# Half of the first batch's maxima in the self attention block, keys and the first queries made earlier

## What is computed

```
x = layernorm(x + self_attention(x))            # causal, one head, then w_proj
x = layernorm(x + cross_attention(x, ctx))      # 16 heads of 8 channels
x = layernorm(x + ffn(x))                       # silu(w1 x) * (w2 x), gelu(h1 .), gelu(h2 .), w3
# cross attention of a batch:
q, k, v = x @ wq, ctx @ wk, ctx @ wv
scores  = q k^T + bias(bucket(source position - target position))   # 16 x 56 x 1500
out     = softmax(scores) @ v @ wo
```

## Time and profile before

| | us |
|---|---|
| median of 3 runs | 994.24 (991.3 to 995.9) |
| the profiled execution | 997.42 |
| its span | 995.6 |
| TensorE busy | 922.1 |
| VectorE busy | 729.7 |
| ScalarE busy | 608.6 |
| GpSimd busy | 376.5 |

### The profile page before, as it was taken

How to read it: one execution, slowest core, us unless ns; L and a number is a source line. 1 busy time by engine, 2 the same in 40 slices (tenths; PEclk the granted TensorE clock), 3 DMA queues, 4 the chain that set the end, 5 groups by cost and what they waited for, 6 DMA issues and landing times.

```text
span 995.6 us, 26073 instructions
## 1 busy us (share of the span) xinstructions
PE 922.1 (93%) x10410; PEld 647.2 (65%) x10410; DVE 729.7 (73%) x1705; ACT 608.6 (61%) x1423; POOL 376.5 (38%) x317
## 2 busy tenths in 40 slices
PE   6766699999999999999999999999999998999996
PEld 3544477767677777676776667777777766555564
DVE  5657778888888888888888888888888884710023
ACT  2322377777777777777777777777777767632232
POOL 7300444455555544444555555544444400000000
PEclk9867899999999999999999999999999999999998
DMA  7729766766666676666666666666677503000001
GB/s 206 243 79 176 178 183 181 200 206 182 180 194 186 188 209 193 197 202 197 194 205 176 182 195 181 193 195 206 203 192 204 151 8 121 1 1 0 1 10 28
DMA packets 56324, 154.96 MB, mean 156 GB/s; under 512 B 23234, under 2 KB 35322, under 8 KB 53114
## 3 DMA queue, kind: packets, MB, share of 16 engines
q1 hardware_dynamic: 55820, 152.44, 53.8%
q10 hardware_dynamic: 384, 0.86, 0.3%
HBM read 110.03 MB, written 42.63 MB: 153 GB/s over the span
## 4 chain that ended last, share of the span: by engine, by line
PE 74%; ACT 7%; DVE 3%; issue 2%; DMA 2%; POOL 1%; SPq 1%; ACTq 0%; DVEq 0%; POOLq 0%
PE ps L113 15%; PE ps L877 12%; PE ps L847 12%; PE ps L603 10%; PE ps L930 8%; PE ps L925 7%; PE ps L886 3%; PE ps L597 2%; ACT e_sb L1060 2%; ACT kpart L1033 2%; ACT k_left L1042 1%; ACT vals L1017 1%; DVE cmax L123 1%; PE ps L613 1%; DMA qst<-qslots 1%
## 5 line engine op out<-in xcount | busy, mean ns | idle before, releaser
L1060 ACT ACTIVATE e_sb<-ps 128x448 f32<-128x448 f32 (+1 forms) x768 | 382.7, 554 | 129.5 <-PE ps L847 68.7
L123 DVE TENSOR_REDUCE cmax<-ps 112x1 f32<-112x512 f32 x512 | 330.8, 680 | 56.8 <-PE ps L113 56.5
L113 PE MATMUL ps<-kst,qst 111*112 111x512 bf16 (+1 forms) x768 | 267.8, 390 | 7.1 <-PEq L132 2.8
L847 PEld LDWEIGHTS ps<-qst,kst 114*128 114x128 bf16 (+1 forms) x3072 | 194.8, 101 | 103.8 <-issue 36.0
L847 PE MATMUL ps<-qst,kst 114*128 114x112 bf16 (+1 forms) x3072 | 229.4, 213 | 15.3 <-ACT e_sb L1060 10.9
L120 DVE CUSTOM_DVE_ANT_0 near_out<-ps,near_nat 112x476 bf16<-112x476 f32 x256 | 157.0, 651 | 37.2 <-PE ps L113 34.6
L1105 POOL TENSOR_TENSOR kpart<-k_left,kpart 128x500 bf16<-128x500 f32 x90 | 102.2, 1136 | 205.4 <-ACT k_left L1042 205.4
L877 PE MATMUL ps<-e_sb,vals 128*32 128x168 f32 (+1 forms) x3072 | 149.5, 312 | 0.0
L1111 POOL TENSOR_TENSOR kpart<-k_left,kpart 128x500 bf16<-128x500 f32 x90 | 125.9, 1399 | 7.1
L113 PEld LDWEIGHTS ps<-kst,qst 111*112 111x112 bf16 x768 | 85.5, 131 | 48.2 <-issue 20.7
L930 PEld LDWEIGHTS ps<-wv,ctxt 128*128 128x128 f32 (+1 forms) x768 | 102.1, 193 | 8.1 <-issue 1.2
(11 more groups left out here) (124 smaller groups left out, 918.9 us busy)
## 6 DMA issues: line engine op xcount, KB each, us to landing
kst<-kparts SPq DMA_DIRECT2D x192, 375.0 KB, 6.8
kparts<-kpart SPq DMA_DIRECT2D x90, 375.0 KB, 2.7
ctxt<-in_ctxT SPq DMA_DIRECT2D x31, 750.0 KB, 8.1
qst<-qslots SPq DMA_DIRECT2D x192, 28.0 KB, 7.1
qslots<-qst SPq DMA_DIRECT2D x4, 672.0 KB, 11.5
kparts<-kst SPq DMA_DIRECT2D x6, 375.0 KB, 3.3
qslots<-kst SPq DMA_DIRECT2D x24, 56.0 KB, 4.4
kst<-in_h SPq DMA_DIRECT2D x1, 1024.0 KB, 5.6
```

The costliest lines, as they stand in the source:

```text
L113: return nc.tensor.matmul(dst[0:TT, 0:hi - lo], m.qst[0:M_ROW, r, p, :], m.kst[0:M_ROW, r, p, lo:hi], start=True, stop=True)
L123: return nc.vector.tensor_reduce(m.cmax[:, r, c, p:p + 1], src[0:TT, 0:BOUND[c + 1] - BOUND[c]], AX.X, ALU.max)
L847: mm = nc.tensor.matmul(st_ps[0:K, w % ST_BANKS, p * TT:(p + 1) * TT], m.kst[0:AUG, u % RING, 4 * h + p, j * P:j * P + K], m.qst[0:AUG, u ...
L1060: nc.scalar.activation(e_sb[0:K, j % E_RING, h * HALF:(h + 1) * HALF], st_ps[0:K, w % ST_BANKS, 0:HALF], ACT.Exp).then_inc(s_ex, 1)
```

## The change

- Maxima 0 to 11 of batch 0 are made in the self attention block: 0 to 3 at the start of step 7, 4 to 7 at the start of step 8, 8 to 11 behind step 8, on TensorE and on VectorE, in two PSUM banks (4 and 5). `max_items` leaves them out of the cross attention block.
- The keys of batch 1 are made at the start of step 6 rather than 5; their split, which VectorE did behind stage 2 of the last group (step 5), stands at the start of step 7, ahead of the first maxima.
- Stage 6 stands earlier within its step, on TensorE, ScalarE and VectorE.
- The bias of the self attention's values is added by ScalarE to the product with the values (the weights of a row sum to one) and no longer by VectorE to the values; the copy of the values out of PSUM goes from VectorE to ScalarE.
- On the sync queue the context of batch 1, `wv` and `sel` are loaded right behind near_nat; the queries of batch 0 are stacked right behind the store of group 0's; the store and stacking of batch 1's keys come behind the store of group 1's queries.

```diff
+SA_MAX = 12
-        bqk, bv, bproj, mask = sb("bqk", [C, 2]), sb("bv", [T, C]), sb("bproj", [TT, C]), sb("mask", [T, T])
+        bqk, bv, bproj, mask = sb("bqk", [C, 2]), sb("bv", [C, 1]), sb("bproj", [TT, C]), sb("mask", [T, T])
-        K_AT, K_BANK = {1: 0, 5: 1}, (6, 2)
+        K_AT, K_BANK = {1: 0, 6: 1}, (6, 2)
+        MAX_AT, MAX_BANK = {7: (0, 4), 8: (4, 8), NG + 5: (8, SA_MAX)}, (4, 5)
# sync queue
-            sp.dma_start(bv[:, :], d["b_v"].broadcast_to([T, C])).then_inc(s_in, 16)
+            sp.dma_start(bv[:, :], d["b_v"].rearrange("o c -> c o")).then_inc(s_in, 16)
...
+            sp.dma_start(m.ctxt[:, 1, :], d["ctxT"][C:2 * C, :]).then_inc(m.s_ctx[1], 16)
+            sp.dma_start(m.wv[:, :], d["wv"]).then_inc(m.s_w, 16)
+            for i in range(2):
+                sp.dma_start(m.sel[:, i, :], d["sel"][i]).then_inc(m.s_w, 16)
...
-            sp.dma_start(m.ctxt[:, 1, :], d["ctxT"][C:2 * C, :]).then_inc(m.s_ctx[1], 16)
-            sp.dma_start(m.wv[:, :], d["wv"]).then_inc(m.s_w, 16)
-            for i in range(2):
-                sp.dma_start(m.sel[:, i, :], d["sel"][i]).then_inc(m.s_w, 16)
-            store_k(1)
             sp.wait_ge(s_q3, 1)
             sp.wait_ge(s_qz[0], 16)
             store_q(sp, m, 0)
+            sp.wait_ge(m.s_qd[0], 16 * 6)
+            stack_q(sp, d, m, 0, 0, m.s_ql[0])
+            sp.wait_ge(s_q3, 2)
+            sp.wait_ge(s_qz[1], 16)
+            store_q(sp, m, 1)
+            store_k(1)
             sp.wait_ge(s_kw, 96)
             sp.wait_ge(s_mem, 3)
             stack_k(sp, d, m, 1, m.s_kl[1])
-            sp.wait_ge(m.s_qd[0], 16 * 6)
-            for n in range(SA_K):
-                stack_q(sp, d, m, n, n, m.s_ql[n])
-            sp.wait_ge(s_q3, 2)
-            sp.wait_ge(s_qz[1], 16)
-            store_q(sp, m, 1)
+            stack_q(sp, d, m, 1, 1, m.s_ql[1])
# TensorE
+            def maxima(first, end):
+                if first == 0:
+                    pe.wait_ge(m.s_ql[0], Q_LOAD)
+                    pe.wait_ge(m.s_kl[0], 96)
+                    pe.wait_ge(s_pte, NG)
+                for n in range(first, end):
+                    if n >= 2:
+                        pe.wait_ge(m.s_mr, n - 1)
+                    max_scores(nc, m, ps[:, MAX_BANK[n % 2], :], 0, n // PAIRS, n % PAIRS).then_inc(m.s_mx, 1)
-            for g, st in schedule((5, 1, 3, 4, 0, 2, 6)):
+            for g, st in schedule((5, 1, 3, 6, 4, 0, 2)):
...
+                if st == "start" and g in MAX_AT:
+                    maxima(*MAX_AT[g])
+            maxima(*MAX_AT[NG + 5])
# ScalarE
-            for g, st in schedule((5, 3, 1, "pt", 4, 0, 6)):
+            for g, st in schedule((5, 3, 6, 1, "pt", 4, 0)):
...
+                    act.wait_ge(s_v, g + 1)
+                    nc.scalar.copy(v[:, g, :, :], ps[0:T, 2:4, :].rearrange("p a (b c) -> p (a b) c", b=4)).then_inc(s_ve, 1)
-                    nc.scalar.copy(at[:, g, :], ps[:, 6, 0:GT]).then_inc(s_oe, 1)
+                    nc.scalar.activation(at[:, g, :], ps[:, 6, 0:GT], ACT.Identity, bias=bv[:, 0:1]).then_inc(s_oe, 1)
# VectorE
+            def maxima(first, end):
+                if first == 0:
+                    dve.wait_ge(s_un, 32)
+                for n in range(first, end):
+                    dve.wait_ge(m.s_mx, n + 1)
+                    reduce_scores(nc, m, ps[:, MAX_BANK[n % 2], :], 0, n // PAIRS, n % PAIRS).then_inc(m.s_mr, 1)
-            for g, st in schedule((2, 1, 4, 0, "x1", 6)):
+            for g, st in schedule((2, 1, 6, 4, "x1")):
...
+                if (g, st) == (7, "start"):
+                    dve.wait_ge(s_kf, 6)
+                    nc.vector.tensor_tensor(kpart[:, 1, :], k_left, kpart[:, 0, :], ALU.subtract).then_inc(s_kr, 1)
...
+                if st == "start" and g in MAX_AT:
+                    maxima(*MAX_AT[g])
-                if st == 0:
-                    dve.wait_ge(s_v, g + 1)
...
-                    if g == NG - 1:
-                        dve.wait_ge(s_kf, 6)
-                        nc.vector.tensor_tensor(kpart[:, 1, :], k_left, kpart[:, 0, :], ALU.subtract).then_inc(s_kr, 1)
...
+            maxima(*MAX_AT[NG + 5])
# cross attention block
-                if live(g, u + lag):
+                if live(g, u + lag) and (u + lag > 0 or n >= SA_MAX):
-                if n == 0:
+                if n == 0 or batch(g, u + lag) == 0:
```

More of the change, by code:

```diff
@@ L435, in _ @@
             dve.wait_ge(s_in, NIN)
-            for g, st in schedule((2, 1, 4, 0, "x1", 6)):
+            for g, st in schedule((2, 1, 6, 4, "x1")):
                 if (g, st) == (1, "start"):
                     dve.wait_ge(s_ld, NLD)
+                if (g, st) == (7, "start"):
+                    dve.wait_ge(s_kf, 6)
+                    nc.vector.tensor_tensor(kpart[:, 1, :], k_left, kpart[:, 0, :], ALU.subtract).then_inc(s_kr, 1)
+                    dve.wait_ge(s_kr, 4)
+                    nc.vector.tensor_tensor(k_left, k_left, kpart[:, 0, :], ALU.subtract).then_inc(s_kr, 1)
+                    dve.wait_ge(s_kr, 5)
+                    nc.vector.tensor_tensor(kpart[:, 2, :], k_left, kpart[:, 1, :], ALU.subtract).then_inc(s_kr, 1)
+                if st == "start" and g in MAX_AT:
+                    maxima(*MAX_AT[g])
                 if st == "start":
@@ L442, in _ @@
                 bc = lambda a: a[:, g, :].unsqueeze(2).broadcast_to([T, GB, T])
-                if st == 0:
-                    dve.wait_ge(s_v, g + 1)
-                    nc.vector.tensor_tensor(v[:, g, :, :], ps[0:T, 2:4, :].rearrange("p a (b c) -> p (a b) c", b=4),
-                                            bv[:, :].unsqueeze(1).broadcast_to([T, GB, C]), ALU.add).then_inc(s_ve, 1)
                 if st == 1:
```

## The result

The changed kernel takes 1006.8 us, the median of 4 runs (1004.43 to 1008.19); the kernel before took 994.21 beside it (991.3 to 995.9). The ratio is 1.0127, with a 95% interval of 1.0095 to 1.016: slower by more than half a per cent, as forecast, and 4.3 us above the predicted 1002.5: inside the stated 994 to 1009, but 0.8 us above the 999 to 1006 that the prediction gave its own sum.

The account below looks back on a forecast made before the run. Bound: engines waiting for each other in self attention, then a chain of waits and query stores in the cross attention's head. Block +9.5, head -1.2: +8.3 us on 997.42, carried to a median of 1002.5; range 994 to 1009.

Parts of the forecast that it names:

- The gain by step 6: Self attention block: early context load, later keys and earlier query projection bring x1 of group 2 to 73.5, 4.5 us earlier.
- Value bias: Self attention: four 1.0 us copies on ScalarE, 0.3 us coming through on VectorE; bias load 0 (-0.5 to +0.5).
- Splits and maxima behind x1 of group 2: Self attention tail: 26.0 us where 11.75 stood, the 14.2 more being 12.2 of work and 2.0 of waiting.
- The head: Start of cross attention: twelve reductions leave, but query stores hold it; loses 0 to 2.4 us, taken as 1.2.
- The sum: Whole kernel: block +9.5, head -1.2, together +8.3 us, so 1005.7 against the profiled 997.42.
- From the profiled execution to the median: Whole kernel: the profiled execution lies 3.2 us over the median 994.24, so the median goes to 1002.5.
- Clock: Rival, self attention: TensorE holds 2.4 GHz in steps 5 to 8; 997.5 to 1000 us; chance 0.13.
- The head gives back more: Rival, cross attention head: quicker stores and landing of the maxima's row give 5.5 us back; 998.2; chance 0.08.
- Splits and maxima find idle time: Rival, self attention: VectorE's gaps take in the 12.2 us of work; 990.5 us, faster; chance 0.09.
- Slower still: Rival: half clock in step 6 and no gain in the head; +12.8, 1007 us; chance 0.10.

Follow-up runs that it names:

- before again: The kernel before, unchanged, profiled once more: 995.29 us (one run).
- e2: Kernel before with only the loads of batch 1's context, wv and sel moved right behind near_nat: 992.53 us, ratio 0.9989.
- e9: Kernel before with 14 idle 128x448 products added on TensorE at the ends of steps 1 to 7: 995.14 us, ratio 1.0013.
- e4: Changed kernel with the value bias load behind the rest of xT, awaited only at step 3 of group 0: 1005.33 us, ratio 1.0114.
- e1: Changed kernel with no maxima in the self attention block, all 24 of batch 0 back in the head: 999.29 us, ratio 1.0059.
- e5: Changed kernel with all 24 maxima of batch 0 in the self attention block: 1015.41 us, ratio 1.0227.
- e3: Changed kernel with the three subtractions that split batch 1's keys on GpSimd, not VectorE: 1005.45 us, ratio 1.0124.
- e7: Changed kernel with group 2's queries stored in the self attention block instead of the head: 1002.85 us, ratio 1.0097.
- the repeats: Both kernels, unchanged, profiled once more: the kernel before 995.29 us, the changed kernel 1007.65 us (one run each).
- e10: Kernel before with both the three waits of e8 taken out and the idle products of e9: 984.37 us, ratio 0.9916.
- e8: Kernel before with early context load, bias not awaited at the start, batch 1's queries stacked in the head: 991.86 us, ratio 0.9982.

## Why the prediction was right, and where it was not

**The gain by step 6: right.** x1 of group 1 came at 64.67 and of group 2 at 74.58, for 63.4 and 73.5. Nearly all of the 1.1 is there before TensorE's first product (1.04), and that is the bias.

**Value bias: mis-sized.** The step priced the new shape of the load "between -0.5 and +0.5, taking 0". It measured +1.04 (9.36 for 8.32): one column of 128 rows lands later than the row that went to 56. That is outside the bounds given, and the other traces widen it: with the column TensorE starts at 9.27 to 9.57 in seven executions, with the row at 6.71, 7.54, 8.32 and 8.73 in four (before again, e2, before, e9). In this execution it came through to x1 of group 2; e4 shows that an earlier start needn't (4.0 us at the start, 1.1 at the block's end). The four copies were 1.00 or 1.01 us, as taken.

**Splits and maxima behind x1 of group 2: right, and the centre of the loss.** 26.2 us for the predicted 26.0; x1 of group 3 after 16.1 of them, as worked out; the wait of TensorE was 6.42 us, for some 5. The step took 3.08 us from group 2's transpose to the end of its projection, from a stretch whose transpose had run at full clock (0.60) though it called that near half; measured were 3.43 (81.37 to 84.80). e1 and e5 price a batch of twelve maxima at 8.6 and 9.0 us of block, where the step had 7.0 of reductions and 2.0 of taking turns. The trace of e3, with no splits in the tail, prices them at 5.2, as the step did. Group 0's queries were stacked in time: TensorE put out the first two maxima from 72.91 on, and VectorE came to them at 79.64.

**The head: right sum, one wrong way.** It gave back 1.4 for the predicted 1.2, which was only the middle between 0 and 2.4. The sync queue's wait ended 14.4 us after the block's start, in the predicted 14 to 16, and that is where the 1.4 came from. The step named the keys as the limit, with the row going out after 17.8 us at the soonest. They came after 17.5 and not 16.3, mostly since the three value products took 6.1 us at 1.2 GHz and not the 4.1 of before, and the row went out after 18.8. But the keys were not the limit: the 6.5 us of landing, which held (6.50), was no fixed cost but what was left of the 9 us behind the context load, so that keys sooner by a us would most likely have made the landing longer by as much. No run here had them sooner with the load in its place.

**The sum.** Block +11.0 for +9.5, head -1.4 for -1.2, the batches and tails -1.4 where nothing was forecast: +8.3. The block's own terms summed to +9.8, and the prediction took 0.3 off without a reason. So the exact agreement is luck: the bias's 1.04 and 0.5 more in the block, against 1.4 in a part which the change doesn't touch and which differs by as much from one execution to the next (table, "rest").

**From the profiled execution to the median.** Here the 4.3 us arose. The prediction carried over that before's profiled execution lay 3.2 above its median. The changed kernel's lay 1.1 below its own. Medians are 12.6 apart, and the repeats 12.4. The execution on which every row of before rests, 997.42, is longer than each of that kernel's 57 timed runs (989.15 to 996.88), so the predicted difference of 8.3 was measured from an unusually long one, and by medians and repeats alike the change costs some 12.5 us. The repeat shows a part of the changed kernel's own spread: 2.9 us more at x1 of group 0 when TensorE has less clock in steps 3 and 4. That this is what the medians contain is argued from two executions of each kernel, not shown.

**The rivals.** *Clock:* step 6 ran at 2.4 GHz, as my sum had it, but the tail stayed at 0.50, so the rival didn't come. *The head gives back more* didn't happen, but its mechanism is real: with half the stores gone from the head (e7) the landing fell to 2.6 us and 3.5 were given back. What it needed was a context load that goes out well ahead of the row, 8.2 us there and 2.6 in the changed kernel. I had put early stores, early load and quick landing in one case, and then, in e7's expectation, denied the half that was true. *Splits and maxima find idle time* fell with the 6.42 us which TensorE waits for VectorE at step 7, and e5 nearly doubles the loss. *Slower still* (1007, chance 0.10) is the number that came nearest to the median, but not by its mechanism: step 6 had full clock and the head gave back 1.4. The repeat shows half clock costing as much in steps 3 and 4 (1007.65).

**Still open:** what the twelve runs of e9 did with their clock; how much of e10's gain is the clock and how much the three waits together with it, since e8 alone gives 1.6 us and e9 none; and the changed kernel with e4, e7 and the idle products together, which wasn't tried.

## What to carry to other kernels

Work moved into an engine's fixed order costs its full time unless it is put where that engine waits for something later than itself: find the latest arrival, and count everything that is serial behind it. Before counting work as removed from a stage, look whether a second chain, here a queue's stores and waits, ends level with it. An earlier start pays only if TensorE keeps its clock in the stretch that follows: removing three waits gave 1.6 us, the same with idle products in the gaps 9.5. And before a sum is built on one profiled execution, look where its time lies among the timed ones.

## What was not expected of the hardware

- TensorE's clock in steps 3 and 4 differs between executions of the same kernel (0.86 and 0.78 granted, or 0.75 and 0.67), worth 2.9 us; with earlier starts or loads it was 0.50 to 0.69 (e2, e4, e8), and with the waits out and idle products in 1.00 (e10), worth 7.5 us of 992. The Trainium skill (TensorE: Matmul & The Clock Gate, What's actually happening) puts the warm-up at under 1% of a typical kernel; the 0.8% here agree, and are more than the effect of most edits tried.
- Two VectorE instructions of 0.39 and 0.63 us took 3.04 and 3.32 beside a subtraction on GpSimd (e3).
- A transfer of 5.2 KB landed in 6.5 us behind 750 and 375 KB of others, and in 2.5 to 2.6 once the first had landed. In twelve traces the small one landed some 9 us after the 750 KB load had gone out, whenever it was itself issued.
- A load of one column into 128 partitions (4 bytes each) made TensorE start at 9.27 to 9.57 in seven traces; the row sent to 56 partitions, 28 KB, let it start at 6.71 to 8.73 in four.
